# Moving the first FFN's weight preparation and the second attention's masks and statistics within a fused attention and FFN kernel

## The chip, the cores and the metric

One Trainium2 chip, one core. The metric is the device time of one launch in microseconds; the kernel before took 795.41 us (median of 3 runs, 794.9 to 795.66). TensorE is PE, VectorE DVE, ScalarE ACT, GpSimd POOL and SyncE SP, as in the profile.

## The reference, cut to what matters

x is 32 x 128 x 128 (batch, rows, features), the context 32 x 77 x 128. Four residual steps run one after the other:

```python
x = x + xattn0(layernorm(x), ctx, mask0)      # 16 heads of 64, rope, softmax, Wo
x = x + ffn0(layernorm(x))                    # one 128x128 product
x = x + xattn1(layernorm(x), ctx, mask1)      # 16 heads of 8, the same mask for all batches
x = x + ffn1(layernorm(x))                    # gated, quantised, inner size 512

# ffn0
scale = max(abs(kernel)) / 7
w = clip(round(kernel / scale), -8, 7) * scale
y = x @ w + bias + (x @ a) @ b                # a: 128x16, b: 16x128
```

The kernel folds a @ b into the quantised w, so that ffn0 is one product with one prepared 128 x 128 matrix. That matrix needs a maximum over all of the raw weights, which crosses partitions, and the product a @ b: both pass through TensorE. It is made once, and it is first used after the last pair of the first attention has begun.

## The kernel before, in words

The 32 batches are taken as 16 pairs p = 0 to 15 of two batches b = 2p + j. Each engine has an instruction stream of its own, written out by hand; semaphores tie the streams together, and there is no scheduler. In the first attention each engine runs `slot(b, p, P, j, more)` twice for each pair. Pairs 0, 1, 14 and 15 are written out, pairs 2 to 13 are a loop of six turns with two pairs in each.

What a slot of the first attention holds on each engine:

- PE, j = 0: `scores` first half, `project_queries` for the next pair, `scores` second half, `score_maxima` for the other batch of the pair, `out_projection(b - 1)`, `turn_maxima`, `values(b)`, then value and query projections for the next pair. PE, j = 1: `scores` and `project_keys` for the next pair in turn with `turn_out(b - 1)`, `out_projection(b - 1)`, `values(b)`, then `score_maxima(b + 1)`, which waits for ACT's last cast of the next pair's keys (`cast_done`), `transposes(p + 2)` and `turn_out(b)`.
- DVE, j = 0: rope of the next pair's queries (L628 and the shuffle L631, four times), `maxima` (L656), `residual` (L674), `normalise` (L662 to L669), `statistics(p + 2)` and `masks(p + 2)`. DVE, j = 1: rope of the next pair's keys (L642 and L644, three times), `normalised_rows(p + 2)` (L607, L609), `residual`, `normalise`, `maxima(b + 1)`, `split_turned(p + 2)` (L618, once a pair).
- POOL: for each group the multiplication of the shuffled half with the sines and the addition (L549, L550 for queries; L558, L559 for keys), and a power for the layernorm (L542).
- ACT: exponentials (L786), casts of roped queries and keys (L772, L777), `fold_in` (L781), copies out of PSUM.

PSUM is eight banks: `pa` is banks 0 and 1 (projections), `ps` banks 2 to 4 (scores), `po` banks 5 to 7 (values, their transposes, the output projection in `po[2]`).

`FfnWeights` makes ffn0's matrix. `row_maxima` (DVE, L146) reduces the rows. `turn` (PE, L169 and L170) transposes the row maxima and `lora_a` into two banks. `quantise` (DVE, L152 to L159) does seven steps. `lora` (PE, L174) multiplies a and b. `add_lora` (DVE, L164) adds the product and signals `ready`. In the kernel before all of it is in pair 1, in the banks `po[1]` and `po[0]`, and since `values` writes these banks, PE's `values` of batch 2 waits for `lora_sbuf` and that of batch 3 for `ready`.

`Layer1Start` holds what the second attention's beginning needs: the statistics of pair 0's rows for ffn0 (L213 to L219), `deviation` (POOL, L223), `rows` (the normalised rows, DVE, L231), and `masks` (L199 to L207). In the kernel before these are in pair 14: statistics and masks at the end of DVE's slot j = 0, `deviation` at the end of POOL's slot j = 0, `rows` in DVE's slot j = 1 between the key ropes.

In pair 15, which has no next pair, generators of the second attention (`next(second)`) put its first steps between those of the first attention: its set-up products (L1607 to L1610) and their copies (L1317 to L1319), `ffn_turn(0)` (L1594), `ffn_project(0)` (L1601, behind `ready`) and so on.

Of the kernel before, what the change touches and what calls it, by code (L numbers as in the profile page):

```python
# [130 lines left out]
class FfnWeights:  # L131
# [3 lines left out]
    def __init__(self, nc, ctx, t):  # L135
        sb = lambda name, shape, dt: ctx.enter_context(nc.sbuf_tensor("f0_" + name, shape, dt))
        self.nc, self.t = nc, t
        self.w_max, self.step, self.inverse = sb("w_max", [D, 1], F32), sb("step", [D, 2], F32), sb("inverse", [D, 1], F32)
        self.lora_aT = sb("lora_aT", [16, D], F32)
        self.row_max, self.max_turned, self.max_read, self.lora_turned, self.lora_sbuf, self.lora_done, self.ready = (  # L140
            ctx.enter_context(nc.semaphore("f0_" + n))
            for n in ("row_max", "max_turned", "max_read", "lora_turned", "lora_sbuf", "lora_done", "w_ready"))
# [6 lines left out]
    def quantise(self, dve, steps, lora_bank, max_bank):  # L149
        vector, w, step = self.nc.vector, self.t["f0"]["w"], self.step  # L150
        dve.wait_ge(self.max_turned, 1)
        steps.link(vector.tensor_reduce(step[:, 0:1], max_bank[:, 0:D], AX, ALU.max))  # L152
        steps.link(vector.tensor_scalar(step[:, 1:2], step[:, 0:1], 1.0 / 7.0, None, ALU.mult))
        steps.link(vector.reciprocal(self.inverse[:], step[:, 1:2]))
        steps.link(vector.tensor_scalar(w[:], w[:], self.inverse[:, 0:1], MAGIC, ALU.mult, ALU.add))
        steps.link(vector.tensor_scalar(w[:], w[:], MAGIC, 7.0, ALU.subtract, ALU.min))
        steps.link(vector.tensor_scalar(w[:], w[:], -8.0, step[:, 1:2], ALU.max, ALU.mult))
        dve.wait_ge(self.lora_turned, 1)
        vector.tensor_copy(self.lora_aT[:], lora_bank[0:16, 0:D]).then_inc(self.lora_sbuf, 1)  # L159

    def add_lora(self, dve, lora_bank):
        w = self.t["f0"]["w"]
        dve.wait_ge(self.lora_done, 1)
        self.nc.vector.tensor_tensor(w[:], lora_bank[:, D:2 * D], w[:], ALU.add).then_inc(self.ready, 1)  # L164

    def turn(self, pe, lora_bank, max_bank):
        tensor, ident = self.nc.tensor, self.t["ident"]
        pe.wait_ge(self.row_max, 1)
        tensor.transpose(max_bank[:, 0:D], self.w_max[:].broadcast_to([D, D]), ident[:]).then_inc(self.max_turned, 1)  # L169
        tensor.transpose(lora_bank[0:16, 0:D], self.t["f0"]["lora_a"][:], ident[:]).then_inc(self.lora_turned, 1)  # L170

    def lora(self, pe, lora_bank):
        pe.wait_ge(self.lora_sbuf, 1)
        self.nc.tensor.matmul(lora_bank[:, D:2 * D], self.lora_aT[:], self.t["f0"]["lora_b"][:], start=True,  # L174
                              stop=True).then_inc(self.lora_done, 1)
# [202 lines left out]
def layer0_attention(nc, ctx, t):  # L378
# [153 lines left out]
    def gpsimd(pool, second):  # L532
# [37 lines left out]
        def slot(b, p, P, j, more):  # L570
            if j == 0:
                if more:
                    for k in range(Q_GROUPS):
                        rope_turn(p + 1, 1 - P, k)
                if more_pre(p):
                    pre(p + 2)
                if pair(p, PAIRS - 2):
                    t["start"].deviation(pool, 0)
            elif more:
                for k in range(3):  # L580
                    rope_keys(p + 1, 1 - P, k)

        pairs_loop(pool, slot, steps, 14)

    def vector(dve, second):
# [117 lines left out]
        def slot(b, p, P, j, more):  # L703
            first = isinstance(b, int) and b == 0
            if j == 0:
                if pair(p, 1):
                    t["ffn_weights"].row_maxima(dve)
                if last_pair(p):
                    next(second)
# [3 lines left out]
                maxima(b + 1, P, 1)  # L713
                if not first:
                    residual(b - 1)
                if pair(p, 1):
                    t["ffn_weights"].quantise(dve, steps, po[1], po[0])
# [10 lines left out]
                if pair(p, PAIRS - 2):  # L728
                    t["start"].statistics(steps, 0)
                    t["start"].masks(dve, steps)  # L730
            else:
# [5 lines left out]
                if pair(p, PAIRS - 2):  # L737
                    t["start"].rows(dve, steps, 0)
# [5 lines left out]
                if pair(p, 1):  # L744
                    t["ffn_weights"].add_lora(dve, po[1])
                if last_pair(p):
                    next(second)
                normalise(b)
                if more:
                    maxima(b + 1, 1 - P, 0)  # L750
                if more_pre(p):
# [103 lines left out]
    def tensor(pe, second):  # L855
# [87 lines left out]
        def values(b, P, j, r):  # L943
# [5 lines left out]
            if isinstance(b, int) and b == 2:  # L949
                pe.wait_ge(t["ffn_weights"].lora_sbuf, 1)  # L950
            if isinstance(b, int) and b == 3:
                pe.wait_ge(t["ffn_weights"].ready, 1)
# [44 lines left out]
        def slot(b, p, P, j, more):  # L997
            first = isinstance(b, int) and b == 0
            if j == 0:
                scores(b, P, j, 0)  # L1000
                if more:
                    project_queries(p + 1, (0,))
                scores(b, P, j, 1)
# [7 lines left out]
                if pair(p, 1):  # L1011
                    t["ffn_weights"].turn(pe, po[1], po[0])
                if last_pair(p):
                    next(second)
# [8 lines left out]
            else:  # L1023
# [12 lines left out]
                if pair(p, 1):  # L1036
                    t["ffn_weights"].lora(pe, po[1])
# [957 lines left out]
```

## Time and profile before

| | us |
|---|---|
| median of 3 runs | 795.41 |
| the profiled execution, as timed | 800.38 |
| its span | 798.5 |
| PE busy | 715.7 (90%) |
| DVE busy | 571.6 (72%) |
| POOL busy | 428.1 (54%) |
| ACT busy | 414.7 (52%) |
| mean granted clock of PE | 0.965 of full |

The first attention ends near 497 us of the span, the second near 670 us, the last FFN at the end. All times below are microseconds from the span's start. In a timeline row the first number is the start, the second the time from the first start to the last end of the instructions that were put together, and the bracket is how long the engine sat idle before it and what released it.

### The profile page before, as it was taken

Reading aid. Unit: us, or ns where it says so; the run is one execution under the profiler, and the core shown is the slowest. Engines: PE = TensorE matmul, PEld = TensorE weight load, DVE = VectorE, ACT = ScalarE, POOL = GpSimd, SP = SyncE. Lnnn points to the kernel's source line nnn. Section 1 sums busy time; section 2 is a strip of 40 time slices with the busy share of each in tenths; the row PEclk is TensorE's granted clock in tenths of the full one; section 3 lists DMA queues with packets and bytes.
Section 4 is the critical chain, followed back from the end, with each engine's and each line's share of the span. In section 5 each row is a group of like instructions: output and inputs, shape, how many; then the busy total and the mean of one; then the engine's idle time right before and its main releaser. Section 6 shows DMA issues by size and latency. Waiting matters only on the chain.

```text
span 798.5 us, 24209 instructions
## 1 busy us (share of the span) xinstructions
PE 715.7 (90%) x9208; PEld 583.9 (73%) x9208; DVE 571.6 (72%) x1597; ACT 414.7 (52%) x879; POOL 428.1 (54%) x494
## 2 busy tenths in 40 slices
PE   2598999999999999999999989999999999867565
PEld 2377878888887888888788868888888888644343
DVE  4566656876786687678668746667676766679996
ACT  2244345444454544445454434656566666448887
POOL 2664535755574575557457544555555555335540
PEclk9799789999999999999999999999999999979989
DMA  9300000000000000000000000000000000000001
GB/s 263 83 10 10 2 10 10 2 8 8 8 0 8 8 0 8 8 8 0 8 0 0 4 8 6 10 11 5 8 4 8 4 8 0 2 1 14 27 26 41
DMA packets 23388, 12.91 MB, mean 16 GB/s; under 512 B 6272, under 2 KB 22480, under 8 KB 23344
## 3 DMA queue, kind: packets, MB, share of 16 engines
q1 hardware_dynamic: 22528, 11.96, 5.5%
q8 instruction: 29, 0.48, 0.2%
q10 hardware_dynamic: 816, 0.36, 0.2%
q14 instruction: 15, 0.12, 0.1%
HBM read 10.21 MB, written 2.10 MB: 15 GB/s over the span
## 4 chain that ended last, share of the span: by engine, by line
PE 36%; POOL 25%; issue 23%; DVE 11%; ACT 2%; POOLq 1%; DVEq 0%; ACTq 0%
POOL a_turned L549 8%; POOL a_qr L550 7%; POOL a_k_turned L558 6%; PE bank L1537 5%; PE bank L1570 4%; POOL a_kr L559 3%; PE bank L1555 2%; PE bank L1513 2%; PE bank L935 2%; DVE f_h_max L1764 1%; PE bank L955 1%; PE bank L1601 1%; PE bank L975 1%; PE bank L1494 1%; PE bank L867 1%
## 5 line engine op out<-in xcount | busy, mean ns | idle before, releaser
L549 POOL TENSOR_TENSOR a_turned<-a_turned,a_rope 128x512 f32<-128x512 f32 x64 | 81.9, 1280 | 175.4 <-DVE a_turned L631 175.4
L786 ACT ACTIVATE a_probs<-bank 77x512 f32<-77x512 f32 x128 | 71.0, 592 | 66.9 <-PE bank L939 66.2
L767 ACT COPY a_vs<-bank 77x512 f32<-77x512 f32 x64 | 37.3, 583 | 105.2 <-PE bank L869 105.2
L628 DVE TENSOR_TENSOR a_straight<-bank,a_rope 128x512 f32<-128x512 f32 x64 | 44.0, 688 | 62.6 <-PE bank L869 58.5
L550 POOL TENSOR_TENSOR a_qr<-a_straight,a_turned 128x512 f32<-128x512 f32 x64 | 82.4, 1287 | 5.0
L656 DVE TENSOR_REDUCE a_am<-bank 128x6 bf16<-128x462 f32 (+1 forms) x96 | 50.3, 580 | 34.4 <-PE bank L913 34.4
L935 PE MATMUL bank<-a_qr,a_kr 64*77 64x128 f32 x1024 | 71.3, 279 | 2.2 <-ACT a_probs L786 0.6
L955 PE MATMUL bank<-a_vs,a_probs 77*64 77x65 f32 x2048 | 69.0, 226 | 3.5 <-DVE f_lora_aT L159 2.0
L955 PEld LDWEIGHTS bank<-a_vs,a_probs 77*64 77x64 f32 x2048 | 64.5, 141 | 7.5 <-issue 3.9
L935 PEld LDWEIGHTS bank<-a_qr,a_kr 64*77 64x77 f32 x1024 | 56.5, 145 | 16.7 <-ACT a_fold L781 8.5
L975 PE MATMUL bank<-a_wo,a_oTn 128*128 128x128 f32 x512 | 64.0, 278 | 0.0
L975 PEld LDWEIGHTS bank<-a_wo,a_oTn 128*128 128x128 f32 x512 | 59.9, 192 | 1.0
L772 ACT CAST a_qb<-a_qr 128x512 bf16<-128x512 f32 x64 | 39.4, 618 | 28.6 <-POOL a_qr L550 28.4
L559 POOL TENSOR_TENSOR a_kr<-a_k_straight,a_k_turned 128x462 f32<-128x462 f32 (+1 forms) x48 | 51.2, 1066 | 3.8
L777 ACT CAST a_kb<-a_kr 128x462 bf16<-128x462 f32 (+1 forms) x48 | 25.6, 534 | 48.9 <-POOL a_kr L559 48.9
L558 POOL TENSOR_TENSOR a_k_turned<-a_k_turned,a_rope 128x462 f32<-128x462 f32 (+1 forms) x48 | 48.0, 1001 | 2.7 <-DVE a_k_turned L644 2.5
L631 DVE STREAM_SHUFFLE a_turned<-bank 128x512 f32<-128x512 f32 x64 | 46.8, 731 | 0.0
L888 PE MATMUL bank<-a_ctxT,a_wk 128*128 128x154 f32 x256 | 43.3, 302 | 2.3 <-DVE a_k_turned L644 1.7
L1417 ACT ACTIVATE a_qr<-bank 128x512 f32<-128x512 f32 (+1 forms) x96 | 43.9, 536 | 1.0 <-PE bank L1555 1.0
L867 PE MATMUL bank<-a_xT_hi,a_wq_hi 128*128 128x256 f32 x128 | 40.0, 312 | 4.8 <-DVE a_xT_lo L618 3.1
L1293 DVE TENSOR_REDUCE a_max_m<-bank 128x8 f32<-128x512 f32 x64 | 41.2, 686 | 4.0 <-PE bank L1518 3.0
L939 PE MATMUL bank<-a_fold,a_fold_w 112*77 112x128 bf16 x512 | 41.0, 223 | 0.0
(254 smaller groups left out, 1922.1 us busy)
## 6 DMA issues: line engine op xcount, KB each, us to landing
out<-x_all SPq DMA_DIRECT2D x8, 256.0 KB, 2.3
x_all<-in_x_dram SPq DMA_DIRECT2D x7, 256.0 KB, 5.3
a_ctx_in<-in_ctx SPq DMA_DIRECT2D x16, 77.0 KB
a_mask_in<-in_mask SPq DMA_DIRECT2D x16, 77.0 KB
a_wv<-in_ctx SPq DMA_DIRECT2D x16, 77.0 KB
a_wq<-in_Wq SPq DMA_DIRECT2D x1, 512.0 KB, 4.7
a_wk<-in_Wk SPq DMA_DIRECT2D x1, 512.0 KB, 6.4
a_wv<-in_Wv SPq DMA_DIRECT2D x1, 512.0 KB, 7.6
```

The lines of the kernel that those rows point to most:

```text
L549: steps.link(nc.gpsimd.tensor_tensor(tv, tv, rope[:, 1:2, :].broadcast_to([128, 4, S]), ALU.mult))
L550: nc.gpsimd.tensor_tensor(qr[P][:, 2 * k:2 * k + 2, :, :].rearrange("p t j s -> p (t j) s"), sv, tv, ALU.add).then_inc(roped, 1)
L558: steps.link(nc.gpsimd.tensor_tensor(tv, tv, rope[:, 3:4, 0:KL].broadcast_to([128, n, KL]), ALU.mult))
L559: nc.gpsimd.tensor_tensor(kr[P][:, lo:hi, :, :].rearrange("p t j s -> p (t j s)"), k_straight[k % 2][:, 0:n * KL], k_turned[k % 2][:, 0:n ...
L628: steps.did(nc.vector.tensor_tensor(straight[k % 3][:].rearrange("p (n s) -> p n s", s=S), pv.rearrange("p (n s) -> p n s", s=S), rope[:, ...
L631: nc.vector.stream_shuffle(turned[k % 3][:], pv, mask=[lane ^ 1 for lane in range(32)]).then_inc(a_free[bk], 1)
L656: nc.vector.tensor_reduce(rows, ps[bk][:, 0:n * KL].rearrange("p (h k) -> p h k", k=KL), AX, ALU.max).then_inc(s_free[bk], 1)
L786: nc.scalar.activation(probs[:, 4 * g:4 * g + 4, :], ps[ST_BANK[g]][0:KL, :].rearrange("p (h s) -> p h s", s=S), ACT.Exp).then_inc(s_free[ ...
L867: nc.tensor.matmul(out, lhs_hi, rhs_hi, start=True, stop=False)
L935: nc.tensor.matmul(ps[ST_BANK[g]][0:KL, i * S:(i + 1) * S], kr[P][e:e + 64, h // 2, j, :], qr[P][e:e + 64, h // 2, j, :], start=i == 0, st ...
L955: last = nc.tensor.matmul(po[r][rows, VW * i:VW * (i + 1)], probs[:, PROBS_SLOT[h], rows], vs[P][:, j, h, :], start=True, stop=True)
L975: last = nc.tensor.matmul(po[2][:, 0:D], oTn[:, i, :], wo[:, i, :], start=i == 0, stop=i == TILES - 1)
```

## The change

Two things are moved; one instruction order inside the moved work changes; nothing is left out.

The first FFN's weights: the row maxima go from DVE's first slot of pair 1 to its last slot of pair 14, behind `maxima(30)`. The rest goes from pair 1 to pair 15, j = 0 (batch 30): PE turns the maxima and `lora_a` between the two halves of the scores, DVE quantises at the start of its slot, PE multiplies a and b behind `out_projection(29)`, and DVE adds the product behind `maxima(31)` and ahead of `residual(29)`. All of it uses `pa[0]`, which no projection of the first attention writes any more; PE waits for its last reader ahead of the transposes. The two waits in `values` go. One semaphore now stands for both transposes, and the copy of the turned `lora_a` comes second of the seven steps instead of last.

The second attention's start: the statistics go from the end of slot j = 0 of pair 14 (DVE) to slot j = 1, between `normalise(29)` and `maxima(30)`; the masks go behind `maxima(30)` and the row maxima; `deviation` (POOL) goes behind the key ropes; `rows` goes to the start of pair 15.

```diff
@@ -137,41 +137,42 @@
         self.nc, self.t = nc, t
         self.w_max, self.step, self.inverse = sb("w_max", [D, 1], F32), sb("step", [D, 2], F32), sb("inverse", [D, 1], F32)
         self.lora_aT = sb("lora_aT", [16, D], F32)
-        self.row_max, self.max_turned, self.max_read, self.lora_turned, self.lora_sbuf, self.lora_done, self.ready = (
+        self.row_max, self.turned, self.lora_sbuf, self.lora_done, self.ready = (
             ctx.enter_context(nc.semaphore("f0_" + n))
-            for n in ("row_max", "max_turned", "max_read", "lora_turned", "lora_sbuf", "lora_done", "w_ready"))
+            for n in ("row_max", "turned", "lora_sbuf", "lora_done", "w_ready"))
 
     def row_maxima(self, dve):
         dve.wait_ge(self.t["later_in"], self.t["later_all"])
         self.nc.vector.tensor_reduce(self.w_max[:], self.t["f0"]["w"][:], AX, ALU.max,
                                      apply_absolute_value=True).then_inc(self.row_max, 1)
 
-    def quantise(self, dve, steps, lora_bank, max_bank):
+    def quantise(self, dve, steps, bank):
         vector, w, step = self.nc.vector, self.t["f0"]["w"], self.step
-        dve.wait_ge(self.max_turned, 1)
-        steps.link(vector.tensor_reduce(step[:, 0:1], max_bank[:, 0:D], AX, ALU.max))
+        dve.wait_ge(self.turned, 1)
+        steps.did(vector.tensor_reduce(step[:, 0:1], bank[:, 0:D], AX, ALU.max))
+        vector.tensor_copy(self.lora_aT[:], bank[0:16, D:2 * D]).then_inc(self.lora_sbuf, 1)
+        steps.wait()
         steps.link(vector.tensor_scalar(step[:, 1:2], step[:, 0:1], 1.0 / 7.0, None, ALU.mult))
         steps.link(vector.reciprocal(self.inverse[:], step[:, 1:2]))
         steps.link(vector.tensor_scalar(w[:], w[:], self.inverse[:, 0:1], MAGIC, ALU.mult, ALU.add))
         steps.link(vector.tensor_scalar(w[:], w[:], MAGIC, 7.0, ALU.subtract, ALU.min))
-        steps.link(vector.tensor_scalar(w[:], w[:], -8.0, step[:, 1:2], ALU.max, ALU.mult))
-        dve.wait_ge(self.lora_turned, 1)
-        vector.tensor_copy(self.lora_aT[:], lora_bank[0:16, 0:D]).then_inc(self.lora_sbuf, 1)
-
-    def add_lora(self, dve, lora_bank):
+        steps.did(vector.tensor_scalar(w[:], w[:], -8.0, step[:, 1:2], ALU.max, ALU.mult))
+
+    def add_lora(self, dve, steps, bank):
         w = self.t["f0"]["w"]
+        steps.wait()
         dve.wait_ge(self.lora_done, 1)
-        self.nc.vector.tensor_tensor(w[:], lora_bank[:, D:2 * D], w[:], ALU.add).then_inc(self.ready, 1)
-
-    def turn(self, pe, lora_bank, max_bank):
+        self.nc.vector.tensor_tensor(w[:], bank[:, 2 * D:3 * D], w[:], ALU.add).then_inc(self.ready, 1)
+
+    def turn(self, pe, bank):
         tensor, ident = self.nc.tensor, self.t["ident"]
         pe.wait_ge(self.row_max, 1)
-        tensor.transpose(max_bank[:, 0:D], self.w_max[:].broadcast_to([D, D]), ident[:]).then_inc(self.max_turned, 1)
-        tensor.transpose(lora_bank[0:16, 0:D], self.t["f0"]["lora_a"][:], ident[:]).then_inc(self.lora_turned, 1)
-
-    def lora(self, pe, lora_bank):
+        tensor.transpose(bank[:, 0:D], self.w_max[:].broadcast_to([D, D]), ident[:])
+        tensor.transpose(bank[0:16, D:2 * D], self.t["f0"]["lora_a"][:], ident[:]).then_inc(self.turned, 1)
+
+    def lora(self, pe, bank):
         pe.wait_ge(self.lora_sbuf, 1)
-        self.nc.tensor.matmul(lora_bank[:, D:2 * D], self.lora_aT[:], self.t["f0"]["lora_b"][:], start=True,
+        self.nc.tensor.matmul(bank[:, 2 * D:3 * D], self.lora_aT[:], self.t["f0"]["lora_b"][:], start=True,
                               stop=True).then_inc(self.lora_done, 1)
 
 
@@ -574,11 +575,11 @@
                         rope_turn(p + 1, 1 - P, k)
                 if more_pre(p):
                     pre(p + 2)
-                if pair(p, PAIRS - 2):
-                    t["start"].deviation(pool, 0)
             elif more:
                 for k in range(3):
                     rope_keys(p + 1, 1 - P, k)
+                if pair(p, PAIRS - 2):
+                    t["start"].deviation(pool, 0)
 
         pairs_loop(pool, slot, steps, 14)
 
@@ -703,18 +704,18 @@
         def slot(b, p, P, j, more):
             first = isinstance(b, int) and b == 0
             if j == 0:
-                if pair(p, 1):
-                    t["ffn_weights"].row_maxima(dve)
                 if last_pair(p):
+                    t["start"].rows(dve, steps, 0)
+                    t["ffn_weights"].quantise(dve, steps, pa[0])
                     next(second)
                 if more:
                     rope_queries(p + 1, 1 - P, 0)
                     rope_queries(p + 1, 1 - P, 1)
                 maxima(b + 1, P, 1)
+                if last_pair(p):
+                    t["ffn_weights"].add_lora(dve, steps, pa[0])
                 if not first:
                     residual(b - 1)
-                if pair(p, 1):
-                    t["ffn_weights"].quantise(dve, steps, po[1], po[0])
                 if last_pair(p):
                     next(second)
                 if more:
@@ -725,29 +726,27 @@
                 if more_pre(p):
                     statistics(p + 2)
                     masks(p + 2, P)
-                if pair(p, PAIRS - 2):
-                    t["start"].statistics(steps, 0)
-                    t["start"].masks(dve, steps)
             else:
                 if more:
                     rope_keys(p + 1, 1 - P, 0)
                     rope_keys(p + 1, 1 - P, 1)
                 if more_pre(p):
                     normalised_rows(p + 2)
-                if pair(p, PAIRS - 2):
-                    t["start"].rows(dve, steps, 0)
                 if last_pair(p):
                     next(second)
                 if more:
                     rope_keys(p + 1, 1 - P, 2)
                 residual(b - 1)
-                if pair(p, 1):
-                    t["ffn_weights"].add_lora(dve, po[1])
                 if last_pair(p):
                     next(second)
                 normalise(b)
+                if pair(p, PAIRS - 2):
+                    t["start"].statistics(steps, 0)
                 if more:
                     maxima(b + 1, 1 - P, 0)
+                if pair(p, PAIRS - 2):
+                    t["ffn_weights"].row_maxima(dve)
+                    t["start"].masks(dve, steps)
                 if more_pre(p):
                     split_turned(p + 2, P)
         pairs_loop(dve, slot, steps, 40)
@@ -946,10 +945,6 @@
                 pe.wait_ge(s_free[ST_BANK[g]], ST_COUNT[g](b) + 1)
             if r == 2 and not (isinstance(b, int) and b == 0):
                 pe.wait_ge(out_added, b)
-            if isinstance(b, int) and b == 2:
-                pe.wait_ge(t["ffn_weights"].lora_sbuf, 1)
-            if isinstance(b, int) and b == 3:
-                pe.wait_ge(t["ffn_weights"].ready, 1)
             for i, h in enumerate(PV_HEADS[r]):
                 for rows in HALVES:
                     last = nc.tensor.matmul(po[r][rows, VW * i:VW * (i + 1)], probs[:, PROBS_SLOT[h], rows], vs[P][:, j, h, :],
@@ -1000,6 +995,10 @@
                 scores(b, P, j, 0)
                 if more:
                     project_queries(p + 1, (0,))
+                if last_pair(p):
+
+                    pe.wait_ge(a_free[0], 6 * PAIRS)
+                    t["ffn_weights"].turn(pe, pa[0])
                 scores(b, P, j, 1)
                 if last_pair(p):
                     next(second)
@@ -1008,9 +1007,8 @@
                 score_maxima(b + 1, P, 1)
                 if not first:
                     out_projection(b - 1)
-                if pair(p, 1):
-                    t["ffn_weights"].turn(pe, po[1], po[0])
                 if last_pair(p):
+                    t["ffn_weights"].lora(pe, pa[0])
                     next(second)
                 turn_maxima(b + 1, P, 1)
                 if last_pair(p):
@@ -1033,8 +1031,6 @@
                 if last_pair(p):
                     next(second)
                 out_projection(b - 1)
-                if pair(p, 1):
-                    t["ffn_weights"].lora(pe, po[1])
                 if last_pair(p):
                     next(second)
                 for r in range(3):
```

## Rows read from the trace of the kernel before

**Rows 1.** The page: busy time by engine, the clock in 40 slices, the chain by engine.
```profile
PE 715.7 (90%) x9208; PEld 583.9 (73%) x9208; DVE 571.6 (72%) x1597; ACT 414.7 (52%) x879; POOL 428.1 (54%) x494
...
PEclk9799789999999999999999999999999999979989
...
PE 36%; POOL 25%; issue 23%; DVE 11%; ACT 2%; POOLq 1%; DVEq 0%; ACTq 0%
```

**Rows 2.** Timeline of DVE: split of turned rows, at pairs 1, 2, 13 and 14.
```profile
68.19 0.42 DVE L618 TENSOR_TENSOR a_xT_lo<-bank,a_xT_hi 128x256 fp32r<-128x256 f32 x1 [0.57 <-ACT a_xT_hi L762]
...
105.29 0.42 DVE L618 TENSOR_TENSOR a_xT_lo<-bank,a_xT_hi 128x256 fp32r<-128x256 f32 x1 [1.28 <-ACT a_xT_hi L762]
...
412.31 0.42 DVE L618 TENSOR_TENSOR a_xT_lo<-bank,a_xT_hi 128x256 fp32r<-128x256 f32 x1 [0.57 <-ACT a_xT_hi L762]
...
440.19 0.42 DVE L618 TENSOR_TENSOR a_xT_lo<-bank,a_xT_hi 128x256 fp32r<-128x256 f32 x1 [0.56 <-ACT a_xT_hi L762]
```

**Rows 3.** Timeline of pair 1 around the first FFN's weights.
```profile
79.19 0.28 DVE L159 COPY f_lora_aT<-bank 16x128 f32<-16x128 f32 x1
79.61 3.16 PE L955 MATMUL bank<-a_vs,a_probs 77*64 77x65 f32 x64 [2.00 <-DVE f_lora_aT L159]
...
94.34 0.48 PE L174 MATMUL bank<-f_lora_b,f_lora_aT 16*128 16x128 f32 x2
...
95.93 0.28 DVE L164 TENSOR_TENSOR f_w<-bank,f_w 128x128 f32<-128x128 f32 x1
...
96.35 2.88 PE L955 MATMUL bank<-a_vs,a_probs 77*64 77x65 f32 x64 [1.53 <-DVE f_w L164]
```

**Rows 4.** Windows, PE alone: stretch, its length, busy (count), clock, DMA share, GB/s.
```profile
80.00:87.00 7.00, 7.00 (x82) 0.52 0.01 2
...
97.00:104.00 7.00, 7.00 (x77) 0.53 0.01 2
...
466.00:469.50 3.50, 3.44 (x24) 0.51 0.00 0
...
475.00:476.00 1.00, 0.56 (x6) 1.00 0.00 0
```

**Rows 5.** Timeline of pair 14, from its last query rope to the next maxima.
```profile
454.25 0.47 DVE L213 BATCH_NORM_STATS2 s_st<-x_all 128x6 f32<-128x128 f32 x2
...
454.60 1.00 PE L888 MATMUL bank<-a_ctxT,a_wk 128*128 128x154 f32 x6
...
455.77 1.27 POOL L550 TENSOR_TENSOR a_qr<-a_straight,a_turned 128x512 f32<-128x512 f32 x1
...
455.90 1.20 DVE L201 TENSOR_SCALAR s_am<-a_mask 128x77 bf16<-128x77 int32 x1
...
457.89 0.63 DVE L642 TENSOR_TENSOR a_k_straight<-bank,a_rope 128x462 f32<-128x462 f32 x1
...
459.20 1.12 POOL L558 TENSOR_TENSOR a_k_turned<-a_k_turned,a_rope 128x462 f32<-128x462 f32 x1 [1.49 <-DVE a_k_turned L644]
...
466.06 1.21 PE L904 MATMUL bank<-a_am,identb 128*128 128x308 bf16 x3 [1.46 <-ACT a_kb L777]
```

**Rows 6.** Timeline: the same maxima and the next scores, an ordinary pair.
```profile
436.87 0.70 PE L904 MATMUL bank<-a_am,identb 128*128 128x308 bf16 x3 [0.65 <-ACT a_kb L777]
...
440.82 1.10 PE L935 MATMUL bank<-a_qr,a_kr 64*77 64x128 f32 x16
```

**Rows 7.** Timeline of pair 15, j = 0 (batch 30).
```profile
471.06 1.10 PE L935 MATMUL bank<-a_qr,a_kr 64*77 64x128 f32 x16
...
473.28 1.10 PE L935 MATMUL bank<-a_qr,a_kr 64*77 64x128 f32 x16 [0.55 <-ACT a_probs L786]
...
475.50 0.23 DVE L1317 COPY a_qr<-bank 112x128 bf16<-112x128 bf16 x1 [5.99 <-PE bank L1610]
...
479.09 0.29 DVE L674 TENSOR_TENSOR x_all<-bank,x_all 128x128 f32<-128x128 f32 x1 [0.37 <-PE bank L975]
...
479.96 0.68 PE L1601 MATMUL bank<-f_w,a_wv 128*128 128x128 f32 x4 [0.63 <-ACT a_wv L1428]
```

## Prediction

> **What bounds the kernel now.** I read the page first. PE is busy 90% of the span, DVE 72%, and the chain that ended last runs through PE (36%) and POOL (25%) [rows 1]. So in an ordinary pair PE has nearly no slack, and what POOL delays is paid by PE. The line of granted clock shows slices of 20 us: it is at nine tenths or more nearly all the time, but the fifth and sixth slices (80 to 120 us) hold 7 and 8 [rows 1]. That is where pair 1 lies, and pair 1 is what the change touches first.
>
> Then I looked for a mark that comes once a pair: DVE's split of the turned rows. It is at 68.19 and 105.29 in pairs 1 and 2, and at 412.31 and 440.19 in pairs 13 and 14 [rows 2]. So an ordinary pair takes 27.88 us and pair 1 takes 37.10 us: 9.22 us too much. The timeline says why. PE's `values` of batch 2 waits 2.00 us for the end of `quantise`, and that of batch 3 waits 1.53 us for the added product [rows 3]. The two waits are only 3.5 of the 9.2 us. The rest is in the windows: after each of them 7 us of fully busy PE run at a mean clock of 0.52 and 0.53 of full, which is the 1.2 GHz level and not the 2.4 GHz one [rows 4]. The same `values` take 3.16 us there.
>
> Pair 14 has a smaller copy of this. PE waits 1.46 us for ACT's last cast of keys ahead of `score_maxima(30)` [rows 5], where an ordinary pair waits 0.65 us [rows 6], and behind it PE is at 0.51 of the clock for 3.5 us [rows 4]. After an ordinary pair's 0.65 us the clock does not fall: pairs 2 to 13 keep nine tenths or more [rows 1].
>
> **Part 1, the weights leave pair 1.** Removed from pair 1: eight DVE instructions, two transposes and one product on PE, and the two waits in `values`. Nothing is put in their place, so pair 1 becomes an ordinary pair: 37.10 - 27.88 = 9.22 us less [rows 2]. As a second reckoning: 2.00 + 1.53 us of waits [rows 3], and two stretches of 7 us at 0.52 of the clock, each worth at most 7 x 0.48 = 3.4 us [rows 4]; that is at most 10.3 us, and less where another engine bounded the stretch. Where the stall goes, what is late next is what is late in an ordinary pair, the cast of keys, 0.65 us. I take 9.2.
>
> **Part 2, pair 14 loses statistics and masks ahead of the key ropes.** Before, DVE works on them from 454.25 to 457.89, and only then begins the first key rope [rows 5]. Its input is ready much earlier: PE's product of 454.60 ends at 455.60. After the change DVE's rope can begin at about 455.7, and its shuffle ends some 1.2 us later (457.89 to POOL's start at 459.20 is 1.31 us) at 456.9. POOL ends the last query rope at 455.77 + 1.27 = 457.04 and now has no power queued behind it, so it begins the keys at about 457.1 instead of 459.20 [rows 5]: 2.1 us earlier. POOL works through the three groups without a gap, so ACT's last cast and the permission for `score_maxima(30)` come 2.1 us earlier too, at about 464.0. That is later than PE could use only by little: PE itself ends its other work at 466.06 - 1.46 = 464.60, and some 0.4 us earlier than that after the change, because `project_keys(2)` no longer waits for DVE's shuffle of the first group. So PE goes on at about 464.2 with no wait to speak of: 1.9 us less.
>
> With the wait gone I expect the clock to stay up. From `score_maxima` to the next batch's scores an ordinary pair takes 440.82 - 436.87 = 3.95 us [rows 6]; pair 14 takes 471.06 - 466.06 = 5.00 us [rows 5, 7]. That is another 1.1 us. Together 3.0 us by batch 30's scores.
>
> **What the moved work costs where it lands.** Statistics now stand ahead of `maxima(30)`. Before they ran from 454.25 to 455.7; in the later slots where POOL leaves DVE alone the same five instructions take about 1 us by my estimate from the first row (0.47 us for both batch statistics) [rows 5]. DVE ends `normalise(29)` at about 464.7, so statistics end at 465.7, and the scores for `maxima(30)` are complete at about 464.2 + 1.2 = 465.4. I take 0.1 us on the path, and 0.8 as the far end (DVE blocked by a POOL addition). The masks' long row, 1.20 us for 128 x 77 [rows 5], is a blocked one: it ends at 457.10, just behind POOL's addition (457.04). After `maxima(30)` POOL is idle until the masks are ready, so masks and row maxima take about 2 us there. The Trainium skill (SBUF — State Buffer, section "Who interferes with whom") says that DVE and GpSimd take their shared ports by a lock for a whole instruction, the loser waiting for its end; the row agrees, and by that rule the moved masks would be about 1 us shorter, and the statistics up to 0.5 us longer if POOL's last key addition were still running.
>
> Who waits for the masks: `masks_ready` at about 469 instead of 458 holds SP's two loads of context, POOL's set-up with `ffn_bias(0)` behind it, and PE's set-up transposes. PE needs it only behind the second half of the scores, where DVE's copy of the result is at 475.50 before [rows 7], 472.5 after. The other two have more slack still, since the first rows that need the bias and the context come behind 477 us.
>
> In batch 30's slot let T be the start of its scores (471.06 before, about 468.1 after). PE's two transposes land in the gap of 0.55 us in which PE waits for an exponential [rows 7]; they cost nothing, and at most 0.3 us if the gap were gone. DVE's `rows` and `quantise` need about 0.6 and 2 us (79.19 + 0.28 against a start some 1.9 us earlier in pair 1) and lie where DVE sat idle for 5.99 us [rows 7]: from T + 1.4 to T + 4.0, while the next DVE work before was at T + 4.44. Slack 0.4 us there and about 1 us more ahead of `maxima(31)`.
>
> The product of a and b is on PE's path: 0.48 us as a pair of rows in pair 1, pipelined [rows 3]; I take 0.3 us. `add_lora` now waits for it at the head of DVE's queue, with `residual(29)`, the next statistics and `ffn_residual(0)` behind. Before, `residual(29)` is at 479.09 and PE's first product that needs the matrix at 479.96, after a wait of 0.63 us for ACT's copy [rows 7]. The addition (0.28 us) [rows 3] and the semaphore fit in that wait; the residual comes 0.5 us later and the next thing it could hold, `values`, is behind 480.
>
> **The sum.** 9.2 + 3.0 - 0.3 = 11.9 us. The profiled execution took 800.38 us (span 798.5): it becomes 788.5. The unprofiled median is 795.41, 4.97 us less than the profiled one; the same 11.9 us are taken from it: 783.5 us. Behind 500 us PE is bound by its own work, so nothing in the trace gives the gain back.
>
> **Rivals.**
>
> A, a fall of the clock in pair 14 or 15 (0.15). Batch 30's slot is full of small gaps: 0.55, 0.44 and 0.63 us on PE, and one window of it is only 0.56 busy [rows 4, 7]. Before, the clock stays at full there. If a gap grows through the new work, or the first fall isn't avoided, PE pays 1.7 us (3.44 us busy at 0.51 [rows 4]) to 3.4 us, plus up to 1 us of wait: 785.2 to 787.9 us. The Trainium skill (TensorE: Matmul & The Clock Gate, section on PSUM-queue depth-cycling) says that frequent short idles between groups of matmuls can make the clock swing between its levels; that speaks for this rival, but the trace shows slot 30 with such idles at 1.00.
>
> B, pair 1 keeps one fall for another reason (0.05): it is written out, not in the loop. 3.4 us back: 787 us. Against it: both falls stand right behind the two named waits.
>
> C, the move does little, because pair 1's excess isn't the waits (0.03): only part 2 is left, 795.41 - 2.7 = 792.7 us.
>
> D, slower than before (0.03). The addition waits at the head of DVE's queue in batch 30's slot, PE then waits for DVE several times in pair 15, and the clock falls after each wait and stays down into the second attention, which is bound by PE. Each microsecond of work at the lower level costs about half a microsecond of the time it takes [rows 4]. To lose the 11.9 us and 1.6 more, PE must spend about 27 us at the lower level. Nothing in the trace holds it there for more than 7 us at a time, so it would take four falls.
>
> **How the numbers follow.** The forecast has 0.74: 783.5 us, with 782.3 to 785.0 as its own range (the ends: no cost for the product and a little more out of pair 14; against it 0.8 us for blocked statistics and 0.3 for transposes). The range for 8 in 10 takes in most of A: 782.3 to 787.0. A measurement of this kernel tells 0.2%, or 1.6 us, from no change. Forecast, A, B and C are all faster by more: 0.96 (something is kept from C); the same 0.01; slower 0.03.
>
> **What the profile after would show.** Right: pair 1 from split to split takes 27.9 to 28.1 us, and windows between 80 and 100 us are at 1.00. First key rope of pair 14 right behind PE's product, POOL's wait ahead of it gone, `score_maxima(30)` with a wait under 0.3 us and no fall behind it. Batch 30's scores some 12.2 us earlier than before. Wrong: a PE wait in pair 15 released by `f_w` or `f_lora_aT`, a clock under 1.00 between 455 and 475 us, or `maxima(30)` waiting for nothing while PE idles.

## The result

| | kernel before | kernel after |
|---|---|---|
| median | 795.41 us | 790.9 us (789.67 to 791.59, 5 runs) |
| ratio | 1 | 0.994 (95% interval 0.9923 to 0.9957) |
| profiled execution | 800.38 us, span 798.5 | 790.74 us, span 788.9 |

The change gains 4.5 us, not 11.9. In a second measurement the same kernel (after_again, below) has 0.9925 (0.9901 to 0.9949), 5.9 us; the first interval takes in that value too. Yet from profile to profile the gain is 9.6 us, close to what was forecast. So the question isn't where the gain went inside the two traces, but why one pair of traces shows 9.6 us and ordinary runs show 4.5 to 5.9.

The page of after, busy time and the clock in 40 slices:

```profile
PE 714.2 (91%) x9208; PEld 583.6 (74%) x9208; DVE 568.3 (72%) x1597; ACT 414.4 (53%) x879; POOL 428.5 (54%) x494
...
PEclk9689999999999999999999999999999999869998
```

The 7 and 8 of the slices from 80 to 120 us [rows 1] are gone. Behind 670 us after has 8 and 6 in the slices near 680 and 700 us, where before has 9 and 7 [rows 1]. Next the timeline of after: the splits at the start and the end of pair 1, then pair 14, then pair 15 (the second column is the duration, the bracket the idle time before and what ended it).

```profile
68.48 0.42 DVE L619 TENSOR_TENSOR a_xT_lo<-bank,a_xT_hi 128x256 fp32r<-128x256 f32 x1 [0.56 <-ACT a_xT_hi L761]
96.21 0.42 DVE L619 TENSOR_TENSOR a_xT_lo<-bank,a_xT_hi 128x256 fp32r<-128x256 f32 x1 [0.55 <-ACT a_xT_hi L761]
...
446.46 0.64 DVE L643 TENSOR_TENSOR a_k_straight<-bank,a_rope 128x462 f32<-128x462 f32 x1 [1.29 <-PE bank L887]
447.84 1.12 POOL L559 TENSOR_TENSOR a_k_turned<-a_k_turned,a_rope 128x462 f32<-128x462 f32 x1
454.76 0.25 PEld L903 LDWEIGHTS bank<-a_am,identb 128*128 128x128 bf16 x3 [0.32 <-ACT a_kb L776]
457.92 0.23 PE L924 MATMUL bank<-identb,a_am 128*112 128x128 bf16 x1 [0.25 <-DVE a_am L657]
...
461.17 1.10 PE L934 MATMUL bank<-a_qr,a_kr 64*77 64x128 f32 x16 [0.33 <-ACT a_probs L785]
466.88 0.48 PE L175 MATMUL bank<-f_lora_b,f_lora_aT 16*128 16x128 f32 x2
467.47 0.29 DVE L165 TENSOR_TENSOR f_w<-bank,f_w 128x128 f32<-128x128 f32 x1 [0.85 <-PE bank L175]
467.67 0.28 DVE L675 TENSOR_TENSOR x_all<-bank,x_all 128x128 f32<-128x128 f32 x1
468.41 0.68 PE L1597 MATMUL bank<-f_w,a_wv 128*128 128x128 f32 x4 [0.63 <-ACT a_wv L1424]
```

Pair 1 takes 96.21 - 68.48 = 27.73 us instead of 37.10 [rows 2]. In pair 14 POOL goes on without a pause from the last query rope to the keys (no bracket at 447.84; the 1.49 us of [rows 5] are gone), and ahead of `score_maxima(30)` only the load of weights still has a wait, of 0.32 us, where PE itself waited 1.46 us before. PE waits 0.25 us ahead of the turned maxima (457.92). In pair 15 the addition (467.47) stands ahead of `residual(29)`, which comes right behind it at 467.67, and `ffn_project(0)` keeps its wait of 0.63 us for ACT. Apart from the 0.25 us that is the picture that the forecast drew. Between 440 and 480 us the clock is at full; later there are stretches where it is not, two of them here:

```profile
440.00:480.00 40.00, 38.23 (x560) 32.48 (x560) 25.13 (x87) 17.48 (x38) 19.03 (x30) 1.00 0.03 8
674.00:684.00 10.00, 7.62 (x72) 5.99 (x72) 5.50 (x23) 3.01 (x7) 1.23 (x4) 0.66 0.00 0
695.00:715.00 20.00, 13.82 (x86) 8.39 (x87) 13.74 (x46) 11.44 (x17) 8.32 (x8) 0.57 0.00 1
```

(Windows of after: stretch, length, busy time and count of PE, PE's weight loads, DVE, ACT and POOL, PE's clock, DMA share, GB/s.)

Read by marks, the 9.6 us between the two profiled executions are (us, from the timelines; "r31" is batch 31's residual, "h0" the first maximum of the last FFN, "end" the end of the last DVE instruction; pairs 2 to 13, 334.90 and 334.79 us, are left out):

| | start to split 1 | pair 1 | pairs 14, 15 (to r31) | r31 to h0 | h0 to end |
|---|---|---|---|---|---|
| before | 68.19 | 37.10 | 57.27 | 218.25 | 79.92 |
| after | 68.48 | 27.73 | 54.92 | 219.73 | 80.35 |
| gain | -0.29 | 9.37 | 2.35 | -1.48 | -0.43 |

### The profile page after: what moved, and what is told of

Read it like the earlier page. It is cut to its first block, busy times and chain, and to the rows that moved or that the text cites. A ratio compares the mean times of both kernels' runs of the same rounds, so it can differ in the third digit from the quotient of the medians.

```text
span 788.9 us, 24208 instructions
## 1 busy us (share of the span) xinstructions
PE 714.2 (91%) x9208; PEld 583.6 (74%) x9208; DVE 568.3 (72%) x1597; ACT 414.4 (53%) x879; POOL 428.5 (54%) x494
## 4 chain that ended last, share of the span: by engine, by line
PE 37%; POOL 26%; issue 22%; DVE 11%; ACT 2%; POOLq 1%; DVEq 0%; ACTq 0%
POOL a_turned L550 8%; POOL a_qr L551 8%; POOL a_k_turned L559 6%; PE bank L1533 5%; PE bank L1566 4%; POOL a_kr L560 3%; PE bank L1551 2%; PE bank L1509 2%; PE bank L934 2%; DVE f_h_max L1760 2%; PE bank L950 1%; PE bank L970 1%; PE bank L1490 1%; PE bank L1597 1%; PE bank L1572 1%
## 5 line engine op out<-in xcount | busy, mean ns | idle before, releaser
L950 PE MATMUL bank<-a_vs,a_probs 77*64 77x65 f32 x2048 | 66.8, 223 | 0.0
L950 PEld LDWEIGHTS bank<-a_vs,a_probs 77*64 77x64 f32 x2048 | 62.4, 137 | 3.9
L1209 POOL TENSOR_TENSOR a_kr<-a_k_straight,a_blocks 128x128 f32<-128x128 f32 x32 | 12.8, 401 | 51.9 <-ACT a_k_straight L1395 51.9
```

What stands on the lines that cost most here:

```text
L950: last = nc.tensor.matmul(po[r][rows, VW * i:VW * (i + 1)], probs[:, PROBS_SLOT[h], rows], vs[P][:, j, h, :], start=True, stop=True)
```

## The experiments

**Is the trace of before an ordinary one?** Its execution took 800.38 us, 4.97 us over the median. The first theory (theory 1 in the expectations) is that it was unusual: the clock falls behind each of its long PE waits, and most executions have fewer or shorter falls. The rival (theory 2) is that pair 1 always costs 37 us and that the gain is given back later. The kernels before and after ran again unchanged.

> The kernel before, unchanged, for a second profile and more times. Theory 1 (the profiled execution that the forecast was summed from was an unusual one: the clock of PE fell behind each of its three long waits, and in an ordinary execution it falls behind fewer): the ratio to the kernel before is 1.000, the profiled execution takes 794 to 798 us instead of 800.38, and pair 1 from split to split takes 31 to 34 us instead of 37.10. Theory 2 (pair 1 is always 37.1 us, the gain was real and is given back behind the first attention in the kernel after): pair 1 takes 37.1 us again and the profiled execution some 800 us.

> The kernel before once more, for its profile. Theory 1 (the length of the lower clock behind the two waits of pair 1 varies): pair 1 takes anything from 32 to 37.1 us; the first wait is 2.00 us every time and always has a fall, of 3.4 or 6.8 us; the second wait is 0.5 to 1.6 us and has a fall only in some executions. Theory 2 (37.1 us is the rule): 37 us.

> As before_third. Over the four profiles of the kernel before, pair 1 is nearer to 33 us than to 37.1 on average, and pair 14 has a fall in one or two of them.

Measured: ratio of before_again 0.9996 (0.9979 to 1.0012), and

| profiled execution | us | pair 1 | lower clock in pair 1 | pairs 14, 15 | r31 to h0 |
|---|---|---|---|---|---|
| before | 800.38 | 37.10 | 13.4 | 57.27 | 218.25 |
| before_again | 794.52 | 33.25 | 6.6 | 56.08 | 216.65 |
| before_third | 795.06 | 32.35 | 3.2 | 56.16 | 218.21 |
| before_fourth | 795.31 | 32.32 | 3.2 | 56.15 | 218.16 |

The fourth column is the time at 1.2 GHz in the pair, worked out as twice (1 - mean granted clock) times the pair. The clock has two digits, so it is good to some 0.3 us; read in windows of 1 us it is 13.6, 6.8, 3.4 and 3.4 us. PE's `values` of batches 2 and 3 in before_again and in before_third, from the timelines:

```profile
80.39 3.29 PE L955 MATMUL bank<-a_vs,a_probs 77*64 77x65 f32 x64 [2.00 <-DVE f_lora_aT L159]
96.12 2.09 PE L955 MATMUL bank<-a_vs,a_probs 77*64 77x65 f32 x64 [0.52 <-DVE f_w L164]
```

```profile
80.44 2.70 PE L955 MATMUL bank<-a_vs,a_probs 77*64 77x65 f32 x64 [2.00 <-DVE f_lora_aT L159]
95.25 2.09 PE L955 MATMUL bank<-a_vs,a_probs 77*64 77x65 f32 x64 [1.16 <-DVE f_w L164]
```

And the windows of PE behind the two waits, again before_again and then before_third (stretch, length, busy, clock, DMA share, GB/s):

```profile
80.00:88.00 8.00, 7.61 (x89) 0.57 0.01 2
96.00:106.00 10.00, 9.88 (x149) 1.00 0.08 20
```

```profile
80.00:88.00 8.00, 7.56 (x105) 0.79 0.01 2
96.00:106.00 10.00, 10.00 (x142) 1.00 0.08 20
```

The first wait is 2.00 us each time, as in [rows 3]. What differs is behind it: 7 us at a clock of 0.52 [rows 4], or 8 us at 0.57, or 8 us at 0.79. So the fall behind the first wait is as long in before_again as in the trace of the forecast, and half as long in the other two. The second wait is 0.5 to 1.2 us and has no fall at all, where the trace of the forecast had 1.53 us and a full fall; and pair 14 has no fall in any of the three, though PE's wait there is 1.41 to 1.44 us against 1.46 [rows 5]. So theory 2 is out: the ordinary pair 1 is 32.3 to 33.3 us. The trace that the forecast used had three falls where these have one. Its time is no single accident (8 of the 48 executions of before that were timed beside these kernels took over 799.5 us), but it isn't the typical one.

> The kernel after, unchanged. Both theories: ratio 0.992 to 0.996. Theory 1: the time from the start to batch 31's residual is near 486 us again and so is the rest, no fall of the clock before 650 us. Theory 2: the part behind 486 us is longer than the same part of the kernel before by 4 us or more.

> The kernel after once more. From batch 31's residual to the last FFN's first maximum the three profiles of before's order had 218.25, 216.65 and 216.65 us, the two of after 219.73 and 217.77. If the change itself lengthens that stretch, it is over 218 us again; if the length there is a matter of where falls happen, it may be anything from 216.6 to 219.8.

Measured: after_again 790.23 us (786.92 to 791.66), ratio 0.9925 (0.9901 to 0.9949), profiled 786.92; after_third 789.21 us. Pair 1 is 27.70 and 27.71 us, pairs 14 and 15 are 54.92 and 54.89: what the change touches is the same to 0.03 us in all three profiles of after, and there is no long wait left in it. The clock falls in its first 60 us, as in every profile here, and then not before 670 us. From r31 to h0 they have 217.77 and 218.82 us. With after's 219.73 their mean is 218.8, and the four of before have 217.8. The spread inside each group is 1.6 to 2 us. Windows of 1 us over all fourteen profiles of this document show where most of it comes from: the time that PE spends at the lower clock in that stretch. It is 7.6 to 7.9 us in before_again, part2_start and product_early, which have 216.65 to 216.67 us from r31 to h0; 11.0 to 11.5 us in six more, which have 218.12 to 218.30; and 16.5 to 16.7 us in after, statistics_behind and wait_short, which have 219.50 to 219.73. Only after_again (6.2 us, 217.77) and after_third (9.2 us, 218.82) are longer than that. Since product_early holds both parts of the change, the change doesn't have to lengthen the stretch. Whether it makes the longer falls more likely (the longest are in three of the nine profiles with the weights moved and in none of the five others), and what the two odd profiles lost, stays open.

**The two parts alone.**

```diff
 part1_weights: the kernel after, with
+ (pair 14, j = 0)  start.statistics; start.masks        # DVE, as before
+ (pair 14, j = 0)  start.deviation                      # POOL, as before
+ (pair 14, j = 1)  start.rows                           # DVE, as before
 part2_start: the kernel before, with these four steps where the change puts them
```

> The first FFN's weights moved as in the change (from pair 1 into pair 15), statistics and masks of the second attention left in pair 14 where they were. Forecast's terms: 9.2 - 0.3 = 8.9 us less, ratio 0.989. Theory 1: the waits of 2.0 and 1.5 us go for certain, the falls behind them only where they had happened: 3 to 5 us less, ratio 0.994 to 0.996. Theory 2: as the whole change, about 0.995, with 9 us gained by the end of pair 1 and lost later.

> Statistics and masks of the second attention moved as in the change, the first FFN's weights left in pair 1. Forecast's term: 3.0 us less, ratio 0.996. Theory 1: 1.2 to 2 us less for certain (the wait), the rest only where the clock had fallen in pair 14: ratio 0.997 to 0.999. Theory 2: 3 us less by the end of the first attention, none of it left in the total.

Measured: part1_weights 791.85 us, ratio 0.9937 (0.9917 to 0.9957); part2_start 793.07 us, ratio 0.9969 (0.9946 to 0.9991). By the marks part 1 alone has pair 1 at 27.70 and pairs 14 and 15 at 56.72; part 2 alone has 32.27 and 54.27. So part 1 gains 4.6 us in pair 1 against the ordinary 32.3, and costs 56.72 - 56.15 = 0.6 us in pair 15. Part 2 gains 56.15 - 54.27 = 1.9 us where the clock had not fallen, and 57.27 - 54.27 = 3.0 us against the trace of the forecast. With both, 54.92 - 54.27 = 0.65 us is again the price of the weights' landing. 4.6 + 1.9 - 0.65 = 5.9 us, which is what after_again measured. Both ratios lie at the lower end of theory 1's ranges or a hair below, and by themselves they are too wide to tell part 2's 1.9 us from the forecast's 3.0.

**What does a PE wait cost, and does the clock always fall?** Pair 1 gives one sample an execution. So three kernels repeat its pattern in each of the twelve looped pairs of the kernel after, as extra work on scratch data.

```diff
 DVE, slot j = 0, behind residual(b - 1), pairs 2 to 13
+    the seven steps of quantise on a scratch tile    # three of them in wait_short
 PE, slot j = 0, ahead of values(b)
+    pe.wait_ge(pad_done, p - 1)                      # not in chain_only
```

> The kernel after, with the seven steps of quantise on scratch data in each of the twelve looped pairs on DVE, at the place where the kernel before has them in pair 1, and nobody waiting for them. Theory 1: PE's wait is what costs, DVE's time is hidden or nearly so: under 1 us a pair, under 12 us in all. Rival (DVE's 1.9 us delays the query ropes and through them POOL and PE): 1 to 2 us a pair, 12 to 24 us in all.

> The same, and PE's values of the pair's first batch wait for the last step, as in the kernel before: twelve waits of 2.0 us in one execution. Theory 1 (whether and how long the clock falls behind such a wait varies from one to the next): some of the twelve have no fall, some 3.4 us and some 6.8 us at the lower level; on average 3.5 to 5 us a pair, 42 to 60 us in all. Theory 3 (the clock falls for 6.8 us behind each wait of 2.0 us, as in the trace of the kernel before): 5.4 us or more a pair, over 65 us in all.

> The same with three of the seven steps, so that PE waits some 1.1 us twelve times. Theory 1: few or none of the twelve have a fall; 1.1 to 2 us a pair, 13 to 24 us in all. Theory 3 (each wait of over a microsecond brings the clock down): 3 us or more a pair, over 36 us in all.

Measured: 804.7, 841.09 and 806.73 us. Per pair, by the splits (pairs 2 to 13 take 334.7 us in the kernel after): chain_only 350.08, so 1.28 us; wait_long 385.90, so 4.27 us; wait_short 351.78, so 1.42 us. Four neighbouring pairs of wait_long, the first splits and the windows between them:

```profile
96.73 0.42 DVE L621 TENSOR_TENSOR a_xT_lo<-bank,a_xT_hi 128x256 fp32r<-128x256 f32 x1 [0.56 <-ACT a_xT_hi L773]
128.57 0.42 DVE L621 TENSOR_TENSOR a_xT_lo<-bank,a_xT_hi 128x256 fp32r<-128x256 f32 x1 [0.57 <-ACT a_xT_hi L773]
161.35 0.42 DVE L621 TENSOR_TENSOR a_xT_lo<-bank,a_xT_hi 128x256 fp32r<-128x256 f32 x1 [0.56 <-ACT a_xT_hi L773]
...
96.76:128.60 31.84, 28.75 (x369) 0.95 0.03 7
128.60:161.38 32.78, 30.21 (x369) 0.90 0.03 7
161.38:193.00 31.62, 28.57 (x369) 0.95 0.02 5
193.00:226.38 33.38, 30.39 (x369) 0.90 0.02 5
```

Each of the twelve pairs has a fall, of 3.2 or of 6.6 us (31.84 x 0.05 x 2 = 3.2; 32.78 x 0.10 x 2 = 6.6; in windows of 1 us 3.4 and 6.8), seven of the shorter and five of the longer, though the work and the wait (2.26 us) are the same. The longer fall costs some 1.2 us more a pair. In wait_short PE waits 1.15 us twelve times:

```profile
PE bank L958 <- DVE a_pad L726: 13.8, 12, 1.2
```

(the waits of PE in wait_short: total, times, longest). Ten of the twelve pairs take 29.1 us and stay at full clock. Two take 30.35 and 30.14 us and have a fall of 3.4 us each. Over all profiles, from pair 1 on in the first attention: waits of 2.0 to 2.3 us (the first wait of pair 1 in five profiles, and wait_long) had a fall 17 times of 17. Waits of 1.4 to 1.53 us (pair 14, and the second wait of pair 1 in the forecast's trace): 2 of 6, both in the forecast's trace. Waits of 1.1 to 1.2 us (wait_short, and the second wait of pair 1 in three profiles): 2 of 15. The 0.65 us of an ordinary pair: never. Theory 3 of the expectations falls for the length of the fall, and theory 1 for its first part: behind 2 us of wait there always is a fall, only its length is open.

chain_only shows the part that the forecast had not seen at all, and here the expectation's rival was right (1 to 2 us a pair) and theory 1 wrong (under 1 us). With no wait and no fall the 1.9 us of DVE work cost 1.28 us a pair, since the two query ropes behind them are late and POOL behind the ropes. POOL's wait for the first of them, in pair 2 of after and then of chain_only:

```profile
107.17 1.29 POOL L550 TENSOR_TENSOR a_turned<-a_turned,a_rope 128x512 f32<-128x512 f32 x1 [1.08 <-DVE a_turned L632]
109.00 1.28 POOL L552 TENSOR_TENSOR a_turned<-a_turned,a_rope 128x512 f32<-128x512 f32 x1 [2.84 <-DVE a_turned L634]
```

So in pair 1 as well a part of the loss most likely came through DVE's queue; no run separates it there.

**What does the landing cost, and can it be had for less?** In the kernel after the product (466.88) lies on PE's path behind the output projection. product_early puts it where PE waits for an exponential in any case:

```diff
 PE, pair 15, j = 0
+    ffn_weights.lora(pe, pa[0])        # ahead of score_maxima(31)
     score_maxima(31); out_projection(29)
-    ffn_weights.lora(pe, pa[0])
 DVE, pair 15, j = 0
+    ffn_weights.add_lora(...)          # ahead of maxima(31)
     maxima(31)
-    ffn_weights.add_lora(...)
```

> The kernel after, with the product of a and b ahead of the second maxima's matmuls of batch 31, where PE waits 0.44 us for an exponential, and its addition on DVE ahead of those maxima, where DVE waits 0.9 us. Theory 1 (the landing in pair 15 costs 0.65 us because the product lies on PE's path behind the output projection): 0.4 to 0.6 us less than the kernel after, batch 29's residual 36.0 us behind pair 13's split instead of 36.67; the ratio, 0.992 to 0.993, can't tell it. Rival (the cost is the two transposes and DVE's quantising, not the product): the residual stays at 36.6.

Measured: 788.89 us, ratio 0.9901 (0.9879 to 0.9923). Residual 29 is 35.90 us behind pair 13's split, as in part2_start where no weights land at all, so the landing's cost was the product with its addition; two transposes and the quantising cost nothing there. But residual 31 is at 55.19, later than after's 54.92. The rows say why, from product_early and then from part2_start, the same place in pair 15:

```profile
479.12 1.08 DVE L1268 TENSOR_TENSOR a_var<-a_mv,a_var 128x2 f32<-128x2 f32 x1
479.13 1.05 POOL L1147 TENSOR_TENSOR a_turned<-a_k_straight,a_blocks 128x512 f32<-128x512 f32 x1
480.65 0.49 PE L1490 MATMUL bank<-a_wv,a_qr 128*128 128x128 f32 x2 [0.88 <-DVE a_wq L1283]
```

```profile
484.83 0.16 DVE L1272 TENSOR_TENSOR a_var<-a_mv,a_var 128x2 f32<-128x2 f32 x1
484.84 1.06 POOL L1151 TENSOR_TENSOR a_turned<-a_k_straight,a_blocks 128x512 f32<-128x512 f32 x1
```

The same addition of two columns takes 0.16 us or 1.08 us. Each time POOL's long operation starts 0.01 us behind it. The Trainium skill (SBUF — State Buffer, section "Who interferes with whom") says that the two engines' shared ports go to one of them for a whole instruction; the trace agrees, 1.08 us being POOL's 1.05. PE then waits 0.88 us for the queries behind it (480.65), and 0.9 us are lost. What decided it can't be read from the starts: in all fourteen profiles the two meet at this place, DVE marked 0.01 to 0.02 us ahead, and in the thirteen others the addition took 0.16 us, also in statistics_behind below, which has product_early's edit. So the 0.9 us are more likely an accident of this one execution than a cost of the edit.

Last, the statistics go behind `maxima(30)`, for the 0.25 us that PE waits at 457.92:

```diff
 DVE, pair 14, j = 1 (beside product_early's edit)
     normalise(29)
-    start.statistics(steps, 0)
     maxima(30)
+    start.statistics(steps, 0)
     ffn_weights.row_maxima; start.masks
```

> The kernel with the early product, and the second attention's statistics behind the maxima of batch 30 instead of ahead of them. In the kernel after the statistics hold those maxima back and PE waits 0.25 us for them ahead of the turned maxima. Expected: that wait gone, batch 29's residual at 35.7 us behind pair 13's split instead of 35.90, ratio to the kernel before 0.989 to 0.992. If the statistics' power on POOL then comes too late for the rows at the start of pair 15, the residual stays at 35.9 or later.

Measured: 787.1 us (786.75 to 789.78), ratio 0.9884 (0.9868 to 0.9901). Residual 29 is at 35.65 us and residual 31 at 54.01, 0.9 us ahead of the kernel after, which is the 0.65 of the product and the 0.25 of the wait; the wait of 0.25 us is gone from PE's timeline. The kernel's interval lies clear of after's in the first measurement (0.9923 to 0.9957); against the second (0.9901 to 0.9949) it only meets the edge. The marks show 0.9 us of the 3.8 us between the two medians. The rest is not explained by the two edits: the profiled executions of one kernel differ by as much (786.92 to 790.74 us for after).

## Why the prediction was wrong, point by point

- **Pair 1, 9.2 us: the mechanism right, the term mis-sized.** The waits go, the clock stays up, the pair becomes an ordinary one (27.7 us). But the ordinary pair 1 of before is 32.3 us, so the term is 4.6 us. The forecast read one profiled execution with 13.4 us at the lower clock in that pair; three more have 3.2 to 6.6. The second reckoning (two waits and two falls) rested on the same trace and couldn't warn. The excess was also not only waits and falls: chain_only has 1.28 us a pair from the DVE steps alone, which the forecast had at nothing.
- **From the profiled execution to the median: the step that failed.** "The same 11.9 us are taken from it" holds only if the 4.97 us between 800.38 and 795.41 lie outside of what the change removes. They lay inside: the second fall of pair 1, the longer first one, and the fall in pair 14 are some 4.8 us in pair 1 (37.10 - 32.3) and 1.1 us in pair 14 (57.27 - 56.15), of which 0.8 us are set off by an early first split (68.19 against 68.97 to 69.10 in the other three). Profiling by itself adds nothing that shows: after's profiled execution (790.74) and before_fourth's (795.31) sit on their medians. Profile to profile the forecast said 788.5 and 790.74 came; that it is so near is no support for the median. With 4.6, 1.9 and 0.65 us for the terms the forecast would have been 789.6 us; the 1.3 us up to the measured 790.9 have no cause shown and lie inside the interval.
- **Pair 14, 3.0 us.** 3.0 against that trace, 1.9 us against the others. The 1.9 us for the wait were right, and the 1.1 us for the fall were there to be had in one execution of four.
- **The landing, 0.3 us.** 0.65 us, the product with its addition. The row of 0.48 us was cut to 0.3 for pipelining, without ground. From the start of `out_projection(29)` to the next product behind it PE takes 2.40 us in after (464.89 to 467.29) and 1.89 us in product_early, so the product is 0.51 us on PE's path, the whole row. The rest is not split up.
- **Statistics ahead of the maxima, 0.1 us.** PE waits 0.25 us there, and 0.25 us are won by moving them. The sum of the forecast leaves out the 0.1 us that its text takes.
- **What hides what.** The transposes in the exponential's gap, `quantise` and `rows` in DVE's idle time, the addition inside the wait for ACT's copy, the masks' long row short without POOL beside it (0.14 us at 458.16 instead of 1.20): all as said.
- **Rivals.** A (a fall in pair 14 or 15) didn't come in any profile of after. B and C are out, pair 1 is clean. D is out. The true case, that the trace itself was dear, was not among them, though the page's 800.38 beside three runs of 794.9 to 795.66 told it. "Nothing in the trace gives the gain back" behind 500 us is the one point left open: 217.8 against 218.8 us on average, most of it by the length of falls near 680 and 700 us.

## What to carry to other kernels

Before a gain is summed from a trace, set the profiled execution's own time against the runs: a surplus of 5 us is work for the reader, and if the trace holds falls of the clock behind waits, look there first: here the surplus was those falls, and it vanished from the gain. Price a wait of PE with its mean fall over several executions, not with the one that the trace shows. And small steps in a queue have a price without any wait: here 1.9 us of DVE work ahead of a rope that POOL waits for cost 1.3 us.

## What the runs showed of the hardware

- The clock's fall behind an equal wait has no fixed length. Twelve equal waits of 2.26 us gave seven falls of 3.2 us and five of 6.6 us (3.4 and 6.8 in windows of 1 us). The Trainium skill (TensorE: Matmul & The Clock Gate, Part 1) says that the monitor's pace is independent of the kernel's start, and that for this reason the point at which the clock changes varies from run to run; the four profiles of before fit that (3.2, 3.2, 6.6 and 13.4 us in pair 1), though none of them shows the reason.
- In this kernel the chance of a fall rises with PE's wait: 2 of 15 at 1.1 to 1.2 us, 2 of 6 at 1.4 to 1.53 us, 17 of 17 at 2.0 to 2.3 us.
- Where DVE and POOL start 0.01 to 0.02 us apart, the same DVE addition of 128 x 2 took 0.16 us in thirteen profiles and 1.08 us in one; the starts don't tell the two cases apart.
